# Second layer of a two-layer image block: image from raw sums, offset convolution in column pieces, sampling weights per half

## The reference, cut to what matters

```
x = x + L0_conv(_ln_c(x));  t = t + L0_ffn(_ln_t(t))      # first layer: deformable conv, 8 experts, top 2
x = x + L1_conv(_ln_c(x));  t = t + L1_ffn(_ln_t(t))      # second layer: below, 8 experts, top 1

def L1_conv(x, ...):                       # G = 4 groups of 16 channels, K = 3
    x = conv_same(x, w_init, b_init)       # 1x1: x @ w_init + b_init, "the image"
    for g in range(G):
        xi = x[..., g, :]
        offsets = conv_same(xi, w_off[g], b_off[g])        # 3x3 -> 18 offsets a pixel
        sampled = sample_with_offsets(xi, offsets, K)      # 9 bilinear samples of a pixel
        h = depthwise_same(sampled, w_dw[g], b_dw[g])      # 3x3
        outs.append(conv_same(h, w_pw[g], b_pw[g]))        # 1x1
```

## Time and profile before

| | us |
|---|---|
| median of three executions | 274.86 |
| their lowest and highest | 274.18, 275.37 |
| the profiled execution | 273.77 |
| its span, first to last instruction | 272.0 |
| PE busy | 230.9 (85%) |
| DVE busy | 191.2 (70%) |
| POOL busy | 136.6 (50%) |
| ACT busy | 60.2 (22%) |
| POOL's 72 sampling products | 57.7 |
| mean granted TensorE clock | 0.986 of full |

### The profile page before, as it was taken

How to read it: one execution, slowest core, us unless ns; L and a number is a source line. 1 busy time by engine, 2 the same in 40 slices (tenths; PEclk the granted TensorE clock), 3 DMA queues, 4 the chain that set the end, 5 groups by cost and what they waited for, 6 DMA issues and landing times.

```text
span 272.0 us, 3157 instructions
## 1 busy us (share of the span) xinstructions
PE 230.9 (85%) x1006; PEld 131.3 (48%) x1011; DVE 191.2 (70%) x480; ACT 60.2 (22%) x102; POOL 136.6 (50%) x195
## 2 busy tenths in 40 slices
PE   0999988987999979979798777789899988999980
PEld 0736467863345623224524233557577856434430
DVE  7797889997894886473506799898877138425486
ACT  1221953210001282614114000101001212311000
POOL 5400009885990619712600899999997002000760
PEclk9999999999999889999999999999999999999996
DMA  3526991000000000000059000000000000000000
GB/s 93 173 69 147 208 227 70 0 2 0 2 0 1 2 1 1 0 0 2 0 123 202 2 4 0 0 2 0 2 0 0 0 2 1 0 2 0 0 19 19
DMA packets 5760, 9.39 MB, mean 35 GB/s; under 512 B 2390, under 2 KB 2926, under 8 KB 5742
## 3 DMA queue, kind: packets, MB, share of 16 engines
q1 hardware_dynamic: 5742, 9.18, 14.5%
HBM read 7.48 MB, written 1.69 MB: 34 GB/s over the span
## 4 chain that ended last, share of the span: by engine, by line
PE 39%; DVE 30%; POOL 16%; issue 7%; ACT 6%; DMA 1%; DVEq 1%; ACTq 0%; POOLq 0%
POOL ring L265 13%; PE ps L1058 5%; PE ps L960 4%; PE ps L810 4%; DVE ps L1225 3%; PE ps L928 3%; PE ps L792 3%; PE ps L986 2%; DVE cm L1172 2%; DVE ring L289 2%; PE ps L725 2%; PE ps L862 2%; POOL big L554 2%; PE ps L840 2%; PE ps L978 1%
## 5 line engine op out<-in xcount | busy, mean ns | idle before, releaser
L265 POOL TENSOR_TENSOR ring<-big 128x384 f32<-128x384 f32 x72 | 57.7, 850 | 16.9 <-DMA big<-pad 16.5
L299 POOL TENSOR_TENSOR big<-big 128x512 f32<-128x512 f32 x30 | 31.9, 1092 | 34.7 <-DMA big<-pad 30.0
L960 PE MATMUL ps<-ring,ident 128*128 128x384 f32 x100 | 36.0, 499 | 8.4 <-POOL ring L265 5.6
L1555 DVE TENSOR_TENSOR ps<-ps,ring 128x384 f32<-128x384 f32 x46 | 25.8, 560 | 6.4 <-PE ps L960 5.1
L960 PEld LDWEIGHTS ps<-ring,ident 128*128 128x128 f32 x100 | 17.7, 190 | 23.1 <-DVE ring L265 5.0
L435 POOL TENSOR_TENSOR rstd<-veps,mhalf 128x4 f32<-128x4 f32 x8 | 8.2, 1027 | 38.9 <-DVE veps L1124 38.8
L792 PE MATMUL ps<-ring,ident 128*128 128x192 f32 x126 | 23.8, 337 | 3.8 <-DVE ring L289 3.6
L792 PEld LDWEIGHTS ps<-ring,ident 128*128 128x128 f32 x126 | 20.1, 190 | 7.6 <-DVE ring L289 7.6
L716 PE MATMUL ps<-zero 128*128 128x512 bf16 (+1 forms) x96 | 21.8, 372 | 0.3 <-issue 0.2
L554 POOL TENSOR_TENSOR big<-big 128x256 f32<-128x256 f32 (+1 forms) x12 | 7.6, 633 | 28.4 <-DVE big L1638 27.8
L265 DVE TENSOR_TENSOR ring<-big,ps 128x384 f32<-128x384 f32 x36 | 19.4, 545 | 0.1
(11 more groups left out here) (282 smaller groups left out, 399.5 us busy)
## 6 DMA issues: line engine op xcount, KB each, us to landing
big<-pad SPq DMA_DIRECT2D x8, 392.0 KB, 9.7
big<-pad SPq DMA_DIRECT2D x8, 240.0 KB, 5.6
w<-in_w_dram SPq DMA_DIRECT2D x2, 512.0 KB
w<-in_w_dram SPq DMA_DIRECT2D x2, 256.0 KB
pad<-img SPq DMA_DIRECT2D x8, 64.0 KB, 2.1
pad<-zero SPq DMA_DIRECT2D x1, 484.0 KB, 3.8
pad<-zero SPq DMA_DIRECT2D x1, 400.0 KB, 4.3
x<-in_x_dram SPq DMA_DIRECT2D x1, 256.0 KB, 2.8
```

The costliest lines, as they stand in the source:

```text
L265: return eng.tensor_tensor(V(ring, 0, slot * SP, [[1, P], [NJ * C, 3], [C1, NJ * G1], [1, C1]]), bigv((py + dy) * SLAB1 + (dx + j0) * C, [ ...
L299: return eng.tensor_tensor(dst, bigv(wy * SLAB0 + wx * C, [C0, J * G0], [1, C0]), table, ALU.mult)
L960: mm(bank(1 + i % 2, 0, P, [1, SP]), ident[:, :], ring[:, slot * SP:slot * SP + SP], start=(n == 0), stop=(n == len(srcs) - 1)).then_inc(s ...
L1555: v.tensor_tensor(acc, acc, ring[:, slot * SP:slot * SP + SP], ALU.add).then_inc(sem("s_add"), 1)
```

## The change

1. **Image from raw sums.** x2 itself is transposed (`image_rows_T`), multiplied by centred weights (`image_rows`; DVE takes the column means off `w_i1` early in the program), and DVE makes `img` from the sum with the reciprocal deviation and the bias, one `scalar_tensor_tensor` a pixel (`image_tokens`). PE turns `img` to channels, into both halves of the partitions (`image_T`). The first half is made inside the loop of the first expert network.
2. **Offset convolution in column pieces.** The image by channel lies in `cm` and in `big` at `MIDDLE`, ten columns a partition row; DVE copies the lower and middle rows, ACT the upper ones. The convolution is six taps on all rows of the array for each of three column sets: INNER (columns 1, 2), OUTER (0, 3), SECOND (4 to 7).
3. **Halves.** Offsets, tents and pair weights are made for columns 0 to 3 and then 4 to 7. POOL starts on the first half's weights.
4. **Slab.** The padded image in DRAM keeps a window of each half row; `img` is written by halves (four DMAs), and the slab is read in two parts: rows 0 to 2 (`slab_top`) and 3 and 4 (`slab_rest`), four DMAs each.
5. **Sums.** In items 0 and 1 PE adds all six of POOL's products, and DVE only its own two. The flag's transpose stands behind PE's sixth addition; the 26 and 6 `idle_columns` ahead of the sampling become 4 and 10, and `keep_clock` goes.
6. **Masks in pairs.** The masks of two experts' pairs follow each other, behind `chosen_hidden`.
7. **Base points moved.** DVE's two additions to `base1` (L1414) go from ahead of the loop of the first expert network to behind units 3 and 5.

```diff
+            def image_columns_out(h):
+                sp.wait_ge(sem("img1"), h + 1)
...
+                sp.dma_start(dst, img[:, HJ * h:HJ * h + HJ, :]).then_inc(sem("pad1_stored"), 16)
...
+                sp.dma_start(dst, img[q:P:2, j0:j0 + R1, :]).then_inc(sem("pad1_stored"), 16)
+            def slab_rows_in():
+                sp.wait_ge(sem("pad1_stored"), 64)
+                for first, rows, arrived in SLAB_PARTS:
+                    for b in range(B):
...
+                        sp.dma_start(V(big, 32 * b, first * SLAB1, [[1, 32], [SLAB1, rows], [1, SLAB1]]), src
+                                     ).then_inc(sem(arrived), 16)

@@ POOL
-            pool.wait_ge(sem("slab1"), 128)
             for i in range(N_ITEMS):
                 for d in S_POOL:
+                    if i < 3:
+                        pool.wait_ge(sem("slab_top" if i % 3 + d // 3 < 3 else "slab_rest"), 16 * B)
                     if i == 0:
                         pool.wait_ge(sem("pairs"), PAIRS.index(d) + 1)
+                    if i == N_ITEMS // 2:
+                        pool.wait_ge(sem("pairs"), K + PAIRS.index(d) + 1)

@@ PE
+            def image_rows_T(h):
+                pe.wait_ge(sem("x_sum"), 2 + h + 1)
+                for j in range(HJ * h, HJ * h + HJ):
+                    last = tr(bank(h, 0, C, [1, P], off=(j % HJ) * P), x2[:, j, :], ident[:, :])
+            def image_rows(h):
+                pe.wait_ge(sem("rawT"), 2 + h + 1)
+                for j in range(HJ * h, HJ * h + HJ):
+                    last = mm(bank(2 + h, 0, P, [1, C], off=(j % HJ) * C), xT[0:C, j, :], w_i1[:, :], start=True, stop=True)
+            def image_T(h):
+                pe.wait_ge(sem("img1"), h + 1)
+                for j in range(HJ * h, HJ * h + HJ):
+                    tr(bank(4 + h, 0, C, [1, P], off=(j % HJ) * P), img[:, j, :], ident[:, :])
+                    last = mm(bank(4 + h, C, P, [1, P], off=(j % HJ) * P), img[:, j, :], ident[:, :], start=True, stop=True)
+            def offset_taps(columns, t0, t1):
+                for t in range(t0, t1):
+                    kt, kx = divmod(t, 3)
+                    pe.wait_ge(sem("middle" if kt else "outer"), needs if kt else 2 * needs)
+                    last = mm(bank(OFF_BANKS[j0 // HJ], 0, 72, [step_j * P, nj], [1, P], off=(j0 % HJ) * P),
+                              w_ob[:, kt, kx, :],
+                              V((big, MIDDLE) if kt else cm, 0, j0 + kx, [[1, P], [step_j, nj], [TILE, P]]),
+                              start=(t == 0), stop=(t == 5))
...
+                if k == HJ + 1:
+                    image_rows_T(0)
                 if k == HJ + 2:
-                    transposes(4, normalised, "xn", 2, [0])
+                    image_rows(0)
+                if k == HJ + 3:
+                    image_T(0)
...
             outputs_by_token(1)
-            keep_clock(4, 7)
...
+            image_rows_T(1)
+            offset_taps(INNER, 0, 1)
+            image_rows(1)
+            offset_taps(INNER, 1, 6)
+            image_T(1)
...
+            offset_taps(OUTER, 0, 6).then_inc(sem("offT_ps"), 1)
+            offset_taps(SECOND, 0, 2)
+            offsets_by_token(0)
+            offset_taps(SECOND, 2, 6).then_inc(sem("offT_ps"), 1)
+            idle_columns(4, 1)
+            offsets_by_token(1)
...
+                    if i == 0 and n == S_POOL_PE(0) - 1:
+                        pe.wait_ge(sem("off_max"), 2)
+                        tr(bank(FLAG_BANK, 0, 1, [1, P]), flagf[:, 1:2], ident[:, :]).then_inc(sem("off_maxT"), 1)
+                        idle_columns(10, 6)
...
             for u in range(E):
-                if u + 2 < E:
+                chosen_hidden(u)
+                if u % 2 == 0 and u + 2 < E:
                     expert_masks(u + 2)
-                chosen_hidden(u)
+                    expert_masks(u + 3)

@@ DVE
+            def image_copies(h):
+                dve.wait_ge(sem("cpad1_zero"), 1)
+                dve.wait_ge(sem("imgT_ps"), h + 1)
+                lower_rows(v.tensor_copy, h).then_inc(sem("outer"), 1)
+                middle_rows(v.tensor_copy, h).then_inc(sem("middle"), 1)
+            def image_tokens(h):
+                dve.wait_ge(sem("rstd"), 5 + h)
+                dve.wait_ge(sem("img1_ps"), h + 1)
+                for j in range(HJ * h, HJ * h + HJ):
+                    last = v.scalar_tensor_tensor(img[:, j, :], bank(2 + h, 0, P, [1, C], off=(j % HJ) * C),
+                                                  rstd[:, j:j + 1], b_i1[:, :], ALU.mult, ALU.add)
...
                 if u == E + 5:
-                    dve.wait_ge(sem("rstd"), 5)
-                    normalise(x2, 1, range(HJ))
+                    image_tokens(0)
+                if u == 2 * E - 1:
+                    image_copies(0)
+                if u in (3, 5):
+                    base_points(1 if u == 3 else 2)
             add_outputs(1)
             moments(x2, range(HJ, J))
             inverse_std(slice(HJ, J), 1e-6)
...
+            image_tokens(1)
+            image_copies(1)

@@ tables
+SLAB_PARTS = ((0, 3, "slab_top"), (3, 2, "slab_rest"))
 def S_POOL_PE(i):
-    return 3 if i < N_ITEMS - 2 else 4
+    return 6 if i < 2 else 3 if i < N_ITEMS - 2 else 4
```

297 lines of the change are left out of this document (155 added, 142 removed).

## The result

| | before | after |
|---|---|---|
| median of four executions, us | 275.06 | 292.52 |
| lowest and highest | 274.18, 275.37 | 291.06, 294.38 |
| profiled span | 272.0 | 291.6 |
| PE, DVE, POOL busy | 230.9, 191.2, 136.6 | 251.9, 192.9, 138.3 |

What follows compares the result with a forecast made beforehand. The prediction took the second layer's sampling, fed by POOL's and DVE's chains, as the bound. Sampling +1.9, clock +0.6 and masks -1.2 gave +1.3 on the profiled 273.77: 275.1, or 276.2 for the median; range 270.8 to 279.3.

Steps and rivals of the forecast that it cites:

- Base points: First expert network: moving DVE's two additions lets the first product start earlier, taken as -0.5 us (0 to -0.6).
- Units 14 and 15: End of the first expert network: the first half's image delays x2's second half from 125.72 to 129.6, +3.9 us.
- Rival (3): Without `keep_clock`, PE's clock falls earlier; image and INNER at half speed delay both chains 1.5 to 2 us: 278; chance 0.10.
- Second image: From x2's second half through the taps: 0.43 us per 256-column tap; DVE's first half of offsets starts at 141.8, 3.1 earlier.
- Rival (2): Taps reading elements 40 bytes apart take double, adding 2.6 + 1.7 us ahead of DVE: 280.5; chance 0.08.
- POOL's start: Ahead of the sampling: the slab's transfer releases POOL at about 145.0, 5.9 us earlier; first pair weights at 144.4.
- DVE's start: D, DVE's first copy for sampling products: 158.3 against 155.76, from 11.7 us of work and 3.6 of waits for POOL.
- Sampling: Second layer's sampling: product 14 waits until 160.8; POOL's end, E, comes at D + 52.6 = 210.9 against 209.05, +1.9 us.
- rival (4): At the sampling, POOL's earlier start is kept whole (-5.9 - 1.2): 267.5 us; chance 0.05.
- Clock: Ahead of the sampling, PE waits and its clock may fall, slowing the first additions: +0.6 us taken (0 to 1.3).
- Masks: Second expert network: the first `chosen_hidden` starts at 230.6 instead of 232.12, -1.2 us (0 to -1.5).
- Rival (1): Tents done in time: D at 155.3 or earlier, 272.5 us, decided at D = 156.9; chance 0.32.

Runs made afterwards that it cites:

- clock_kept: The changed kernel with eight idle matmuls in PE's gap before the last pair of outputs: 290.34 us, ratio 1.059 to the kernel before.
- all three edits: The changed kernel with ACT's first-half tents ahead of its second-half activation, taps over contiguous columns, and idle matmuls in PE's gap: 276.40 us, ratio 1.006.
- clock_second: The kernel with all three edits, plus twelve idle matmuls ahead of the flag's transpose and 22 instead of ten behind it: 276.60 us, ratio 1.005.
- the best version: With all three edits, POOL holding its seventh product, idle columns around the flag, first image half behind units 14/15, ten idle matmuls there: 270.84 us, ratio 0.984.

## Why the prediction failed, and where it held

**Base points** (-0.5): without the 0.5 that stood ahead of them, the first products ran 0.6 us earlier and x2's first half 0.4, and the same with this edit alone; by the times it measures -0.7 with no change inside the interval. Held.

**Units 14 and 15** (x2's second half at 129.6 less the 0.5 of the base points, 129.1): 132.05. From x2's first half it was 8.1 us before, 15.4 in the change and 12.6 with the clock kept, alone and with all three edits. So at full clock the term is +4.5 for the +3.9 forecast, and 2.8 of the miss are the clock's. The sum put no clock risk here. Rival (3) did ("short work and waits from 122 to 132"), with 0.10 and 1.5 to 2 us; it was true, and its price was 3.7, or 6.5 with taps that follow the clock.

**Second image**: the tap's price, 0.43 for 256 columns, half of "a full-array tap of 512 costs 0.85", is the step that failed most. That price came from taps with contiguous runs of sixteen. The new ones step 40 bytes and took 1.80 and 0.90. Rival (2) named it, with 0.08, and priced it at 4.3 us; it cost D 8.8. Its 4.3 counted OUTER and the two SECOND taps ahead of the first half's offsets, but the four behind them (3.8 us) count too: in the changed kernel ACT's second activation waits for them and the first half's tents stand behind it, and with ACT's order turned DVE itself still waits 2.37 us for the second half's offsets. The argument for a price near zero, that 32-bit numbers take 1.67 ns a column anyway, fell. The rule that the prediction set beside it, of the Trainium skill (SBUF — State Buffer, Door 1: The DMA port swizzle), that a step over more than 16 bytes is penalised, agrees with these runs; they show 4 and 40 bytes and nothing between.

**POOL's start** (144.5 after the base points, set by the slab): 162.59. The prediction followed transfers and the first half's offsets, and gave ACT's tents 0.6 us of work; it did not read where they stand in ACT's queue, behind an activation of the second half. No rival had this. The edit that turns the order was worth 4.5 us of D, and 2.3 beside contiguous taps. With all three edits POOL starts at 144.30, but released by the pair weight, which the prediction had 0.6 ahead of the slab; the number held, the mechanism did not.

**DVE's start** (D = 158.3): 176.44, and 158.06 with the three edits. Within that term the work was 10.6 us for the 11.7 forecast, and the waits for POOL 4.1 for 3.6. The sentence on the two clipping operations, that by the Trainium skill (SBUF — State Buffer, Who interferes with whom) they would wait as well, came true: 0.49 and 0.94 where they take 0.31 and 0.30 alone. That is the 0.8 it said.

**Sampling** (product 14 at 160.8, "what counts is D and not POOL's start"): with the three edits it starts at 160.86. E - D was 53.9 for 52.6, and 52.8 in clock_second, where the clock stayed full. (The terms as they are written add up to 52.2 and not 52.6, and rival (4)'s 274.86 - 7.1 is 267.8 and not 267.5; both are small beside the miss.) "What counts is D" held in ten of the eleven kernels of the table, and fails where POOL starts 1.6 us ahead of D.

**Clock** at the sampling (+0.6 of at most 1.3): 1.3, the upper end.

**Masks** (-1.2): 1.7 in the profile after, 2.2 (1.2 to 3.2) alone.

So the sum stood for a kernel with contiguous taps, a full clock and ACT's tents in their place. That kernel was built and takes 276.40 us, the forecast 276.2. That they agree so closely is luck in part. In its profile the terms miss by +0.6 (x2's second half), +1.0 (from there to the first half's offsets), -0.6 (from there to D), +0.9 (E - D with the clock's 0.6) and -0.5 (the masks), 1.4 us in all, and this execution's front part was 1.3 us ahead beyond the base points. The failures are one price taken from a row of another access pattern, one queue not read, and one clock rival given too little chance and price. Rival (1), the tents in time, needed D below 156.9: it came about only when POOL was held back.

What stays open: how much of the stride's price depends on the step's size, why the clock's fall near 94 to 104 comes at different places, why the clock fell in clock_kept while PE worked without a pause on strided taps, and why the executions of the same instructions are about 1 us apart at x2's first half where no clock fell.

## What to carry to other kernels

When work is split into halves so that a third engine can start early, write down the queue of every engine in between, also those with little work: one instruction of the second half ahead of the first half's undoes the split. Take a matmul's price from a row with the same access pattern of its moving operand, not only the same number of columns. And before removing idle matmuls, look at what PE will do in the stretch behind them: here three waits of 0.5 to 0.7 us in a row, or one of 2.2, cost 3 us and more, not much less than the 4.2 that the best version gains in all.
